# The residual added by TensorE in PSUM, with statistics read from PSUM, for the first two batches

## What is computed

```python
def _time_mix_layer(x, ln_w, ln_b, Wk, Wv, Wr, Wo):
    normed = _layer_norm(x, ln_w, ln_b)
    k = jnp.einsum('btd,ed->bte', normed, Wk)
    v = jnp.einsum('btd,ed->bte', normed, Wv)
    r = jax.nn.sigmoid(jnp.einsum('btd,ed->bte', normed, Wr))
    kv = k * v
    # state = 0.95 * state + 0.05 * kv, token by token
    y = r * states
    return x + jnp.einsum('btd,ed->bte', y, Wo)
...
x = _layernorm(x + two_layers(x))
x = _layernorm(x + experts(x))
```

## Time and profile before

| | us |
|---|---|
| median of 3 runs | 375.12 |
| lowest and highest | 375.1, 377.2 |
| the profiled execution | 376.44 |
| its span, first to last instruction | 374.6 |
| head, up to the first product of the experts | 93.2 |
| TensorE busy | 334.0 |
| VectorE busy | 262.8 |
| ScalarE busy | 170.0 |

### The profile page before, as it was taken

How to read it: one execution, slowest core, us unless ns; L and a number is a source line. 1 busy time by engine, 2 the same in 40 slices (tenths; PEclk the granted TensorE clock), 3 DMA queues, 4 the chain that set the end, 5 groups by cost and what they waited for, 6 DMA issues and landing times.

```text
span 374.6 us, 7109 instructions
## 1 busy us (share of the span) xinstructions
PE 334.0 (89%) x2295; PEld 283.8 (76%) x2295; DVE 262.8 (70%) x851; ACT 170.0 (45%) x311; POOL 194.4 (52%) x236
## 2 busy tenths in 40 slices
PE   6979768587899999999999999999998999998942
PEld 3444454245896987999879699999997899998842
DVE  6486954758984887787778878987535787775224
ACT  1535425444554464455545445545555444553100
POOL 4021216862315555225454766856877557877722
PEclk9999969999999999999999999999999999999976
DMA  7912991525002211521111435213138312112141
GB/s 202 221 43 71 102 288 44 168 71 142 3 19 75 66 43 33 139 64 33 46 43 39 172 99 139 63 46 97 61 92 207 68 31 77 30 46 54 37 151 56
DMA packets 61245, 32.59 MB, mean 87 GB/s; under 512 B 15995, under 2 KB 58823, under 8 KB 61210
## 3 DMA queue, kind: packets, MB, share of 16 engines
q1 hardware_dynamic: 55866, 23.96, 26.8%
q0 software_dynamic: 4256, 7.94, 7.2%
q10 hardware_dynamic: 1088, 0.26, 0.3%
HBM read 19.01 MB, written 13.69 MB: 87 GB/s over the span
## 4 chain that ended last, share of the span: by engine, by line
PE 67%; DVE 9%; POOL 8%; issue 8%; ACT 4%; DMA 3%; DVEq 0%; POOLq 0%; ACTq 0%
PE ps_o L779 16%; POOL returned L1463 4%; PE bank L624 3%; PE pair1h L708 3%; PE bank L632 3%; PE bank L634 3%; POOL picked L1486 2%; PE ps_o L649 2%; PE pair0g L762 2%; PE pair1g L762 2%; DVE kv_sb L1085 2%; PE bank L740 2%; PE bank L604 2%; PE pair0g L763 2%; PE pair0g L764 2%
## 5 line engine op out<-in xcount | busy, mean ns | idle before, releaser
L779 PE MATMUL ps_o<-proj_sb,hidden 128*104 128x128 f32 x768 | 96.2, 273 | 0.2 <-DVE o_sb L1266 0.2
L1446 POOL DMA_INDIRECT slot_rows<-x_rows,row_to x64 | 71.3, 1114 | 42.6 <-DVE prod L1254 24.3
L779 PEld LDWEIGHTS ps_o<-proj_sb,hidden 128*104 128x104 f32 x768 | 90.2, 170 | 1.1 <-issue 0.7
L948 ACT ACTIVATE gate_s<-pair0g,bgate_sb 128x308 f32<-128x308 f32 x64 | 33.1, 517 | 73.6 <-PE pair0g L764 73.6
L1486 POOL DMA_INDIRECT picked<-expert_rows,row_from x48 | 50.3, 1048 | 31.1 <-DVE prod L1254 19.3
L1254 DVE SCALAR_TENSOR_TENSOR prod<-pair1h,bfc_sb,gate_s 128x308 f32<-128x308 f32 x64 | 34.0, 531 | 22.8 <-ACT gate_s L948 22.8
L955 ACT ACTIVATE hidden<-prod 128x616 f32<-128x616 f32 x64 | 45.5, 711 | 8.7 <-DVE prod L1254 8.7
L1254 DVE SCALAR_TENSOR_TENSOR prod<-pair0h,bfc_sb,gate_s 128x308 f32<-128x308 f32 x64 | 34.1, 533 | 14.6 <-ACT gate_s L948 14.1
L948 ACT ACTIVATE gate_s<-pair1g,bgate_sb 128x308 f32<-128x308 f32 x64 | 32.9, 514 | 24.0 <-PE pair1g L764 23.4
L1418 POOL TENSOR_SCALAR shifted<-moments 128x4 f32<-128x4 f32 x24 | 5.5, 230 | 69.0 <-DVE moments L1042 68.8
L762 PE MATMUL pair1g<-slotT_hi,gate_hi 128*128 128x308 f32 x64 | 26.0, 406 | 2.7 <-DVE prod L1254 2.6
(11 more groups left out here) (201 smaller groups left out, 771.9 us busy)
## 6 DMA issues: line engine op xcount, KB each, us to landing
slot_in<-slot_rows SPq DMA_DIRECT2D x20, 260.0 KB, 3.5
expert_rows<-o_sb SPq DMA_DIRECT2D x24, 156.0 KB
x_in<-in_L_attn_h SPq DMA_DIRECT2D x4, 512.0 KB, 5.1
x_rows<-in_L_ffn_w_gate SPq DMA_DIRECT2D x8, 256.0 KB, 4.4
x_rows<-in_L_ffn_w_c_fc SPq DMA_DIRECT2D x8, 256.0 KB, 5.3
proj_sb<-in_L_ffn_w_c_proj SPq DMA_DIRECT2D x8, 256.0 KB, 6.0
out<-picked SPq DMA_DIRECT2D x12, 128.0 KB, 2.4
slot_rows<-slot_in SPq DMA_DIRECT2D x5, 260.0 KB, 7.2
```

Of the source, the lines that this page charges most:

```text
L779: mm = nc.tensor.matmul(ps_o[0:PART, P * part:P * part + P], hidden[:, e % 2, c, PART * part:PART * part + PART], proj_sb[:, e, c, :], sta ...
L948: nc.scalar.activation(gate_s[:, c % 2, :], pair[c % 2][0][:, 0:COLS], ACT.Identity, bias=bgate_sb[:, e, j:j + 1]).then_inc(g_copied, 1)
L1446: nc.gpsimd.indirect_dma_start(out=slot_rows, out_offset=bass.IndirectOffsetOnAxis(ap=row_to[:, c:c + 1], axis=0), in_=x_rows[:, b, c // K ...
```

## The change

For batches 0 and 1 alone, the residual is no longer added by VectorE:

- TensorE gets a stage `carry` ahead of each of the eight output products. It multiplies the identity with the residual, tile by tile, into the bank of the product: x_in in layer one, x_in and x_mid in layer two. The product then accumulates on top (start is false there).
- The product's bank is no longer `ps_o` but the bank that held v of the same half (bank2 for even halves, pair1g for odd ones), save for batch 1, half 3, which keeps `ps_o`. So a carry waits until VectorE has read v.
- VectorE's statistics read the sum from PSUM. Its adds and skip sums for these batches are gone, and the last statistics of batch 1 stand ahead of its slots.
- ScalarE gets a stage `added` that copies the sum from PSUM to SBUF. It waits for the product and for the statistics of it; the norm now waits for the copy, and so do the v product two halves on and the carries of layer two.

```diff
-TENSOR_HEAD = [("turn", 0, 0), ("kvr", 0, 0), ("turn", 0, 1), ("kvr", 0, 1), ("out", 0, 0), ("split", 0, 0),
+TENSOR_HEAD = [("turn", 0, 0), ("kvr", 0, 0), ("turn", 0, 1), ("kvr", 0, 1), ("carry", 0, 0), ("out", 0, 0), ("split", 0, 0),
...
             if b >= 2:
                 return bank[1 + n % 2]
-            return ps_o
+            if (b, n) == (1, 3):
+                return ps_o
+            return mix_banks(b, n)[2]
...
+                if b < 2 and c > between:
+                    pe.wait_ge(x_added, c - between)
...
+            def carry(b, n):
+
+                c = step(b, n)
+                if (b, n) == (1, 3):
+                    pe.wait_ge(rows_made, 1)
+                else:
+                    pe.wait_ge(kv_made, c)
+                if n == 0:
+                    pe.wait_ge(x_loaded[b], 16)
+                if n > 1:
+                    pe.wait_ge(x_added, step(b, n - 2))
+                ps = out_bank(b, n)
+                for j in range(HT):
+                    t = HT * (n % 2) + j
+                    nc.tensor.matmul(ps[:, P * j:P * j + P], ident[:, :], x_in[:, b, t, :],
+                                     start=(j == 0), stop=False, skip_group_check=True)
+                    if n > 1:
+                        nc.tensor.matmul(ps[:, P * j:P * j + P], ident[:, :], x_mid[:, b, t, :],
+                                         start=False, stop=False, skip_group_check=True)
...
-                if b < 2 and c > 1:
-                    pe.wait_ge(x_added, c - 1)
-                if b == 1 and n == 0:
-                    pe.wait_ge(rows_made, 1)
...
-                                          w_mix[:, 3 * L + n // 2, :], start=True, stop=True)
+                                          w_mix[:, 3 * L + n // 2, :], start=(b > 1), stop=True,
+                                          skip_group_check=(b < 2))
...
+            def added(b, n):
+
+                last = (n + 2) // 4
+                act.wait_ge(stats_made[last], step(b, n + 2))
+                act.wait_ge(out_made, step(b, n))
+                dst = x_mid if n < 2 else x_in
+                nc.scalar.activation(dst[:, b, HT * (n % 2):HT * (n % 2) + HT, :],
+                                     out_bank(b, n)[:, :].rearrange("p (j d) -> p j d", d=P), ACT.Copy)\
+                  .then_inc(x_added, 1)
...
-                if norm > 0:
+                summed = norm > 0 and b < 2
+                if summed:
+                    dve.wait_ge(out_made, step(b, n - 2))
+                elif norm > 0:
                     dve.wait_ge(x_added, step(b, n - 2))
...
-                    i = nc.vector.bn_stats(stats[:, r, norm, j, :], source_of(b, n)[:, j, :])
+                    i = nc.vector.bn_stats(stats[:, r, norm, j, :],
+                                           out_bank(b, n - 2)[:, P * (j % HT):P * (j % HT) + P] if summed
+                                           else source_of(b, n)[:, j, :])
...
+                if b < 2 and n > 1:
+                    dve.wait_ge(x_added, step(b, n - 2))
```

46 lines of the change are left out of this document (23 added, 23 removed).

## The result

The changed kernel takes 385.96 us (median of 4 runs, 384.69 to 387.21) against 375.15 for the kernel before: 1.0269 times as long, 95% interval 1.024 to 1.0298. The forecast was 380.7 us, with a range up to 383.3. The sign is right, and the loss is 10.8 us instead of 5.6. Ratios here leave out an execution that is over 1.5% above the fastest of its kernel; there is one, in the last experiment.

A forecast was written before the change was run, and what follows sets the result against it. A full TensorE bounds the kernel behind 100 us, a TensorE-ScalarE-VectorE chain the head. Terms -0.2 + 4.4 + 0.4 + 0.8 + 0.9 - 0.7 = +5.6 on 375.12 give 380.7 us; range 378.8 to 382.0, to 383.3 with rival 1.

The forecast's parts named there:

- The chain: Head, round TensorE, ScalarE and VectorE: batch 0's logits, choice and rows 4.2 us late; all terms sum to +5.6 us.
- ScalarE's order: Batch 0, second layer: `added 0, 2` ahead of `high 2` holds up split 2, 0; 2.8 of the +4.4 us.
- batch 0's carries: Batch 0, second layer: identity matmuls on TensorE, 1.76 us per carry, give 1.6 of the +4.4 us.
- Batch 1: Both layers up to the first product of the experts: terms +0.4, +0.8, +0.9 and -0.7 us, 1.4 in all.
- the copy `high 6` behind `added 1, 1`: Batch 1, first layer: ScalarE's weight copy comes 0.5 us later and TensorE waits for it, +0.4 us.
- The statistics from PSUM: VectorE's statistics reading PSUM: four cost 0.04 us by the trace, taken as nothing; the skill page would give 0.26 us.
- The clock: TensorE's granted clock: taken as 0, bounds -1.4 to +1.8 us, the gap of 1.68 us having cost nothing.
- The new gap: Rival 1: clock falls in the gap at 38.8 to 41.6 ahead of split 2, 0; +1.8, 382.5 us, chance 0.18.
- The old slow stretch at the routing: Clock at 0.50 from 50 to 56 us behind the logits: no cost as it is, -1.4 us if it did not come.
- every later stage moves by the same: First product of the experts at 98.8 instead of 93.17, every later stage moved by the same.
- Rival 2: Less carried through: ScalarE's order costs less or slack behind the head absorbs part; 377.9 us without the order's 2.8, chance 0.10.
- Rival 3: Faster: VectorE's chain is the bound, carries lie in TensorE's waits; batch 0 gains 4.6 us, 370.5 us, chance 0.04.

The follow-up runs named there:

- the last experiment: Kernel before with VectorE's second-half scan ahead of the first add, products in v's banks: 371.88 us, 0.9891; with batch 1's last statistics ahead of VectorE's slots: 372.16 us, 0.9925.
- the second profile: Changed kernel run again without an edit: 386.84 us, ratio 1.0279 to the kernel before; its profiled execution took 385.3 us.
- the copy moved: Changed kernel with ScalarE's copy `added 0, 2` put behind the weight copies `high 2`: 380.61 us, ratio 1.013 to the kernel before.
- the first and third: Profiles of the unedited changed kernel: the first from the 385.96 us measurement, the third from a later repeat at 384.61 us, ratio 1.022.
- the filled kernel: Changed kernel with 11 matmuls on ones in the 2.65 us gap ahead of split 2, 0: 382.42 us, ratio 1.0179 to the kernel before.
- Filling both gaps of the changed kernel: Changed kernel with 11 matmuls on ones ahead of split 2, 0 and 3 + 12 in batch 0's routing: 382.21 us, ratio 1.0178 to the kernel before.

## Why the prediction was right in sign and wrong in size

**The chain: right.** Measured from the first k, row_to comes 4.36 us later (forecast 4.2), of which ScalarE's order is 2.9 (2.8) and batch 0's carries 1.6 (1.6). Batch 1 loses 1.37 us (1.4) apart from the clock, and the copy `high 6` behind `added 1, 1` shows in TensorE's wait of 2.21 us where it was 1.72, 0.5 for the forecast's 0.4. From the end of the last product to the first product of the experts there are 4.27 us (4.4). Taking back the order and half of the second layer's carries together takes back nearly all of the loss (1.0018). All these terms are within 0.2 us of the forecast.

**The statistics from PSUM: right.** Four take 0.89 us against 0.87. By form they are 285 ns against 278, the same count of elements from PSUM and from SBUF:

```profile
L1072 DVE BATCH_NORM_STATS2 stats<-x_in 128x6 f32<-128x128 f32 x48 | 10.3, 278 | 1.5 <-DMA x_in<-in_L_attn_h 1.5
...
L1072 DVE BATCH_NORM_STATS2 stats<-bank 128x6 f32<-128x128 f32 x16 | 3.6, 285 | 3.2 <-PE bank L668 3.2
```

The 65 ns that the Trainium skill (VectorE: DVE Perf Modes, section on the TRN2 errata) would lead to, an estimate, are not there.

**The clock: wrong.** The step that failed is "The clock of TensorE [...] I take 0, the gap of 1.68 being nearest in kind". It was sized at nothing, and what stands beyond the chain measured 4.0 us: 9.6 us over the three measurements of the changed kernel, less the 5.6 of the chain. It failed in three places.

1. The new gap. I gave its fall a chance of 0.18 and a price of 1.8 us. It came in one of three profiles of this kernel and in four of six with the gap left empty; filled, the kernel is 2.9 us faster on average, and no low execution is left, though not all of that is the fall behind the gap, as said there. In the second profile the first fall took 1.8 us up to row_to (50.39 against 48.55), as priced; behind it a shorter stretch at the routing (3.69 us from k to the split) gave 1.5 back and the further fall at 78 took more, so that the head is 3.1 us longer in all. The second fall need not follow from the first: with the copy moved it comes without it, and costs as much (2.8 us). The clock stayed at 1.00 over the gap of 1.68 us in every profile of a kernel that has it, but it was no measure for one of 2.65. The Trainium skill, TensorE: Matmul & The Clock Gate, Part 1, with the low clock as the default, gives the fall if the gap counts as idle; the second profile agrees (0.69 from 42 to 46), the first and third don't (1.00).
2. The old slow stretch at the routing. I took it as moving with the work. It moved by 7.0 us where the routing moved by 4.4, and so covers less of the routing and more of k, v and r: k to the split is 5.17 and 5.09 us in the two profiles without a fall in the gap, against 3.87 and 3.75. That is 1.3 us. My bounds had -1.4 to +1.8, but for other events; that the stretch could cover more of k, v and r was none of them, though the trace of the kernel before would have bounded it: with all three at half clock, at the step from 54.19 to 56.04 shown above, they take 3 x 1.85 = 5.5 us, 1.7 more than 3.87.
3. Behind 100 us I said that every later stage moves by the same. Two of three profiles lose 1.8 to 2.5 us at the slot load near 292 us, from a fall behind the wait, and in the first from a wait 0.9 us longer (in the third, 1.85 us, it is hardly longer than the 1.73 of the kernel before). What brings this on, whether the shifted place of the scatters against other transfers or the execution, stays open.

The ledger, against the kernel before: of the 9.6 us, filling the gap takes back 2.9. The 6.7 that the filled kernel still loses lie in its head, which is 6.7 us longer (87.73 against 81.02): 4.2 up to row_to, 1.5 in the rest of batch 1, which is the chain as forecast, and 1.0 in k to the split (4.87 against 3.87), the moved stretch.

The range had a slip of its own: 380.7 less 1 and 1.4 is 378.3, and plus 1 is 381.7, not 378.8 and 382.0. Nothing hangs on it.

Rival 2 did not come: from the first product of the experts to the end the kernel before takes 281.4 and 279.7 us and the changed one 283.0, 281.3 and 282.6, so nothing of the head's loss is taken up there. Rival 3 fell with the split waiting for `added 0, 2` just as its condition said, but what it priced was real: the scan ahead of the add, without carries and with the products in the banks of v, gives 4.1 us.

## What to carry to other kernels

When a change opens an idle stretch on TensorE in dense work, price it twice: the gap itself, and a fall of the clock over the work behind it, which here comes in some executions only. Filling a gap of 2.65 us gave 2.9 us on average without shortening the chain. And where VectorE is late, first ask whether the order of its list does it: moving the scan ahead of the add in each layer, with the product in another bank, gained 1.1%, while moving the add itself to another engine put its cost and a new loop through ScalarE on the path and lost 2.6%.

## What the runs showed of the hardware that I had not expected

- The same gap of 2.65 us, behind the same work, is followed by a lower granted clock in one execution (0.69 from 42 to 46 us) and not in another (1.00).
- Fills that keep the clock at 1.00 where they stand need not pay: in the kernel before they took the slow stretch at 50 to 57 us away, the profile had one at 73 to 80 us, and the kernel became 0.6% slower. Filling both gaps of the changed kernel gained nothing over filling one (1.0178 and 1.0179). A fall near 78 us came in four profiles, with fills (0.55 and 0.50) and without (0.57 and 0.50).
- The slow stretch at the routing is 6.8 us long in the kernel before and in the changed one, and its place is not tied to the work: it moved by 7.0 us where the work moved by 4.4. Two programs that are alike for their first 50 us (the kernel before, and the change in batch 1 alone) have k to the split 0.9 to 1.5 us apart, each in two profiles.
